# Output projection moved into the recurrence, two token norms merged into their neighbours by halves, in a convolution, recurrence, attention and experts kernel

## The chip, the cores and the metric

The kernel runs on one core of one Trainium2 chip. A core has five engines with a queue each: PE (matrix products into PSUM, 8 banks of 512 fp32 columns by 128 partitions), DVE (vector), ACT (scalar functions), POOL (general, slow), and SP, which issues the DMAs. They meet only through semaphores. The metric is the device time in microseconds of one execution; lower is better. Three runs of the kernel before gave 5703.51, 5706.22 and 5708.03, median 5706.22.

## What is computed

Four images (B = 4) of 128 channels by 64 x 64 positions (L = 4096 tokens, C = 128). Cut to what matters here:

```
order   = patches (4 x 4 pixels, 256 of them) sorted by a score from two convolutions
x1      = x in that order, plus a position table;  x1n = layernorm(x1)
xm, z   = x1n @ in_proj.T                  (256 channels each)
xc      = silu(causal conv over 4 tokens of xm)
h[t]    = exp(dt[t] A) * h[t-1] + dt[t] B[t] xc[t]      (256 x 16 states)
y[t]    = (sum over states h[t] C[t] + D xc[t]) * silu(z[t])
out_m   = y @ out_proj.T                   (128 channels), put back in the image's order
t1      = x + out_m                        (residual, tokens by channels)
q, k, v = layernorm(t1) @ W_qkv;  q and k normed over the tokens
t1      = t1 + softmax(10 q k.T) v @ W_out + b_out      (4 heads of 32)
out     = t1 + experts(layernorm(t1))      (8 experts, best 2 by router)
```

## The kernel before, in words

`program` runs `setup` once and then a loop over the four images. The body is a row of blocks: `score_and_sort`, `project`, `scan`, `unsort`, `qkv`, `attention` with `attention_out`, `ffn`. At a block's end `k.clear` is a barrier of all engines that also clears the semaphores, so nothing of one block overlaps the next. All data of an image lies in SBUF, in one arena of 44032 fp32 columns, at hand-written offsets; the order of work on each engine is written out by hand.

**`scan`** is the recurrence: 8 chunks (`NCH`) of 512 tokens (`CH`), 16 states each (steps s = 0 to 15), two halves of 128 channels. In a step PE spreads row B of the state over all partitions (L967, bf16, bank 0), may do some side work (`side`: parts of softplus for the next chunk, and `lend`, L922, which spreads B early for states 3, 6 and 10), spreads row C of two steps earlier (L919, bank 1), and adds the state of six steps earlier to y by identity matmuls (`total`, L913, banks 6 and 7; at its state 0 the D term comes first, L911). ACT writes exp(dt A) into banks 3 to 5 (L1004), saves the last column of a state (L1007), copies C (L990) and the lent rows (L996). DVE makes dt x B (`inject`, L1098), which reads bank 0, and runs the scan proper (L1122), two per step, one injection between them. POOL multiplies the states by C (L1067) in a ring of 8 buffers, and makes the injections of the three lent states (L1056). `finish` (L1104, DVE) multiplies y by silu(z), in place in `sz`, in step 4 of the following chunk, and after everything for the last one. Bank 2 (`X_BANK`) is shared by the side work. An fp32 matmul is two passes in the profile, one instruction each; a bf16 matmul and a transpose are one. All queues are in order.

**`unsort`**: SP loads the image anew (2 MB). PE projects y to 128 channels in 32 token tiles, two fp32 matmuls each, y being the stationary operand with a stride of 16 columns (L1171); ACT copies the eight banks to `om` (L1191). POOL puts the image into patch order (L1163). Then PE, for each of the eight groups of four tiles, applies the transposed permutation (two matmuls of 512 columns, L1179) and adds the image by four matmuls with the identity (L1183), which makes them tokens by channels; it waits for all of `om` first. DVE copies a group to `t1` (L1197) and takes the statistics of its four tiles (`tile_stats`, L1208).

**`qkv`** begins with `normalize`: DVE aggregates 32 tiles (L1225), adds eps (L1227), ACT takes the root (L1222), DVE the reciprocal (L1229) and then all 32 normalised tiles (L1232); PE transposes them (L1279), ACT copies the eight banks to `tnt` (L1315). When all are there PE starts on k and q (L1289), ACT keeping and squaring each (L1319, L1320).

**`attention_out`**: PE projects the output by channels (L1645), ACT adds the bias as it copies (L1657), PE transposes (L1650), DVE adds to `t1` (L1663) and takes the statistics (L1208). **`ffn`** begins with the same `normalize` and transposes (L1757), copies (L1811), then router (L1764, L1814, L1770), gates (L1838 to L1862, DVE) and experts (L1777, added by L1872).

## Time and profile before

| what | value |
|---|---|
| median of three runs | 5706.22 us |
| profiled execution: its time, its span | 5710.99 us, 5708.9 us |
| granted clock over the span | 0.943 |
| busy over the span: PE, DVE, ACT, POOL | 4840.9, 4925.1, 3936.4, 1610.3 us |
| first image: recurrence | 205 to 667 us |
| first image: unsorting, then norm up to the first key projection | 667 to 720, 720 to 733 us |
| first image: rest of `qkv`, attention | 733 to 784, 784 to 1321 us |
| first image: `attention_out`, `ffn` | 1321 to 1345, 1345 to 1440 us |

A line of the order of time gives start, duration, engine, line, operation, output<-input, count and, in brackets, how long the engine had been idle and who released it. A line of a stretch gives each engine's busy time and PEclk, the share of TensorE's full clock (2.4 GHz) that was granted. The images follow each other some 1430 us apart and look alike, so one of them is read.

### The profile page before, as it was taken

The numbers are of one execution on the slowest core, as the hardware profiler recorded it, in microseconds if no ns is written. First come the engines' busy times: TensorE is split into PE (matmuls) and PEld (weight loads), VectorE is DVE, ScalarE is ACT, GpSimd is POOL, SyncE is SP. The second block draws the span as 40 slices with busy tenths as digits, with TensorE's granted clock in tenths as the row PEclk, the third lists the DMA queues.
The fourth block names the chain that finished last, engine by engine and source line by source line (L and its number), as shares of the span: only waits on it lengthen the run. The fifth ranks groups of instructions, "written<-read, shape, count | busy, mean of one in ns | idle before, by whom it ended". The sixth has DMA issues, their size and how long they took to land. (4 is left out here: it accounts for less than half of the span.)

```text
span 5708.9 us, 100723 instructions
## 1 busy us (share of the span) xinstructions
PE 4840.9 (85%) x34256; PEld 2049.1 (36%) x34328; DVE 4925.1 (86%) x6398; ACT 3936.4 (69%) x5625; POOL 1610.3 (28%) x790
## 2 busy tenths in 40 slices
PE   5788879998788887999878887799986888879997
PEld 2333433333333343333433334333343333433334
DVE  6799679998789967999868996799986899679998
ACT  3777468993477837999347783789924777379992
POOL 1488500000048850000004884000000588400000
PEclk9899989999889998999988999899988899989998
DMA  1000020000000002000000000200000000020000
GB/s 40 0 1 0 15 64 9 9 5 23 23 0 1 0 15 64 9 9 5 23 23 0 1 0 15 64 9 9 5 23 23 1 1 0 15 64 9 9 5 15
DMA packets 41638, 87.27 MB, mean 15 GB/s; under 512 B 11672, under 2 KB 27872, under 8 KB 38112
## 3 DMA queue, kind: packets, MB, share of 16 engines
q1 hardware_dynamic: 41184, 81.11, 5.3%
q8 instruction: 298, 4.88, 0.4%
q14 instruction: 156, 1.28, 0.1%
HBM read 26.55 MB, written 8.39 MB: 6 GB/s over the span
## 5 line engine op out<-in xcount | busy, mean ns | idle before, releaser
L1483 ACT ACTIVATE arena<-ps 128x1024 f32<-128x1024 f32 x2048 | 1913.4, 1033 | 196.9 <-PE ps L1446 183.7
L1512 DVE TENSOR_TENSOR arena<-arena 128x1024 f32<-128x1024 f32 x1664 | 1901.5, 1216 | 35.0 <-ACT arena L1483 34.4
L1122 DVE TENSOR_TENSOR_SCAN arena<-ps,hlast,arena 128x512 f32<-128x512 f32 x1024 | 1251.3, 1265 | 26.5 <-ACT hlast L1007 12.1
L1067 POOL TENSOR_TENSOR arena<-arena 128x1024 f32<-128x1024 f32 x512 | 1200.7, 2355 | 241.0 <-ACT arena L990 173.0
L1446 PE MATMUL ps<-arena 128*32 128x512 f16 x16384 | 1097.4, 384 | 124.7 <-issue 46.7
L1429 PE MATMUL ps<-arena 128*32 128x512 f32 x8192 | 1071.3, 601 | 7.6 <-ACT arena L1483 3.9
L913 PE MATMUL ps<-arena,ident 128*128 128x512 f32 x2048 | 965.4, 595 | 1.1
L1004 ACT ACTIVATE ps<-arena,amat 128x512 f32<-128x512 f32 x1024 | 705.1, 689 | 372.2 <-DVE arena L1122 365.3
L1446 PEld LDWEIGHTS ps<-arena 128*32 128x32 f16 x16384 | 468.3, 98 | 982.1 <-issue 640.9
L1826 POOL MEMSET arena<- 128x1024 f32 x4 | 3.8, 952 | 2646.1 <-POOLq L101 2646.1
L1098 DVE TENSOR_TENSOR arena<-arena,ps 128x1024 f32<-128x1024 f32 x416 | 497.2, 1195 | 86.1 <-remote 62.6
L913 PEld LDWEIGHTS ps<-arena,ident 128*128 128x128 f32 x2048 | 392.3, 192 | 345.3 <-issue 316.6
L1429 PEld LDWEIGHTS ps<-arena 128*32 128x32 f32 x8192 | 212.4, 109 | 417.7 <-ACT arena L1483 237.3
L990 ACT ACTIVATE arena<-ps 128x512 f32<-128x512 f32 x512 | 297.0, 580 | 14.0 <-PE ps L919 11.9
L1872 DVE SCALAR_TENSOR_TENSOR arena<-ps,arena 128x128 f32<-128x128 f32 x1024 | 274.0, 342 | 1.6 <-PE ps L1777 0.2
L967 PE MATMUL ps<-arena,sel 128*128 128x512 bf16 x376 | 149.4, 397 | 147.9 <-DVE arena L1098 142.6
L1777 PE MATMUL ps<-expw,arena 128*128 128x512 f32 x512 | 250.9, 616 | 12.2 <-DVE arena L1841 8.3
L919 PE MATMUL ps<-arena,sel 128*128 128x512 bf16 x480 | 189.1, 394 | 83.0 <-ACT arena L990 79.0
L486 PE MATMUL ps<-arena 128*128 128x512 f32 x512 | 233.5, 617 | 18.3 <-DVE arena L346 18.3
L1056 POOL TENSOR_TENSOR arena<-arena 128x1024 f32<-128x1024 f32 x96 | 226.6, 2360 | 8.6 <-ACT arena L996 8.6
L602 PE MATMUL ps<-arena,ident 128*128 128x512 f32 x448 | 222.7, 610 | 0.4
L1416 PE MATMUL ps<-arena,ones 128*32 128x512 f32 x1536 | 203.6, 603 | 2.9 <-DVE arena L1512 1.7
(257 smaller groups left out, 4578.5 us busy)
## 6 DMA issues: line engine op xcount, KB each, us to landing
arena<-x SPq DMA_DIRECT2D x32, 512.0 KB, 5.2
arena<-arena SPq DMA_DIRECT2D x64, 256.0 KB, 6.0
arena<-arena SPq DMA_DIRECT2D x64, 224.0 KB, 5.8
arena<-arena SPq DMA_DIRECT2D x28, 512.0 KB, 3.5
arena<-pe SPq DMA_DIRECT2D x256, 32.0 KB, 1.8
out<-arena SPq DMA_DIRECT2D x8, 1024.0 KB, 3.9
expw<-L_ffn_expert_w SPq DMA_DIRECT2D x1, 512.0 KB
wqkv<-L_attn_W_qkv SPq DMA_DIRECT2D x1, 192.0 KB
```

Source lines behind the costliest of these rows:

```text
L913: last = pe.matmul(k.bank(Y_BANK + h), k.ident[:, :], halves(hb[s % RING])[:, h, :], start=False, stop=s == DS - 1)
L990: act.activation(cs[s % 4], k.bank(C_BANK), ACT.Copy).then_inc(cs_s, 1)
L1004: act.activation(da(s, h), halves(dt[q])[:, h, :], ACT.Exp, scale=k.amat[:, h, s:s + 1]).then_inc(da_s, 1)
L1067: pool.tensor_tensor(halves(hb[s % RING]), halves(hb[s % RING]), cs[s % 4].unsqueeze(1).broadcast_to([128, HD, CH]), ALU.mult).then_inc(hc ...
L1098: dve.tensor_tensor(halves(dbx[(q + owned(s)) % 2]), halves(u[q]), k.bank(B_BANK).unsqueeze(1).broadcast_to([128, HD, CH]), ALU.mult).then ...
L1122: dve.tensor_tensor_scan(halves(hb[s % RING])[:, h, :], da(s, h), halves(injected)[:, h, :], k.hlast[:, s, h, :], ALU.mult, ALU.add).then_ ...
L1429: last = pe.matmul(k.ps[32 * h:32 * h + 32, O * CH:(O + 1) * CH], v[:, j * 128 + 32 * h:j * 128 + 32 * h + 32], probs[(2 * j + h // 2) % 8 ...
L1446: last = pe.matmul(k.ps[32 * t:32 * t + 32, (2 * group[p] + e) * CH:(2 * group[p] + e + 1) * CH], ks[:, h, j * 128 + 32 * t:j * 128 + 32 * ...
L1483: act.activation(probs[p % 8], k.bank(2 * group[p], 2 * CH), ACT.Exp, scale=SCALE / SPLIT ** 2).then_inc(exp_s, 1)
L1512: dve.tensor_tensor(acc[p % 2], acc[p % 2], probs[p % 8], ALU.add).then_inc(acc_s, 1)
L1777: pe.matmul(k.bank(expert_bank(i, hb)), tnt[:, i * 128:(i + 1) * 128], k.expw[:, hb * HE:hb * HE + HE, :].rearrange("p e c -> p (e c)"), s ...
L1872: dve.scalar_tensor_tensor(tile, k.bank(expert_bank(i, hb), C, e * C), gate[:, i, hb * HE + e:hb * HE + e + 1], tile, ALU.mult, ALU.add).t ...
```

## The change

Three parts. First, `scan` projects each finished chunk to 128 channels itself: in step 12 of the next chunk, PE in bank 2, ACT back into `sz`; the last chunk after all sums. The lend of state 3 moves from step 13 to 14, ACT's copies of the lent states 3 and 6 to between the two exponentials of steps 14 and 15. Second, `unsort` only transposes the projected chunks (32 transposes with the strided columns as the stationary operand), and takes in the norm that `qkv` had. Groups go in the order 0, 4, 1, 5, 2, 6, 3, 7, so that each merge needs only two banks of `om`. The norm goes in two halves of 16 tiles; of each half DVE normalises the even tiles and ACT the odd ones (as x times scale plus shift). Third, `attention_out` is gone: `ffn` multiplies the attention's output, as the stationary operand, by `W_out` straight into tokens by channels, with the bias added by a bf16 matmul of ones (three bf16 pieces of the bias in rows 0, 32 and 64), and norms by halves in the same way.

```diff
 setup:
-    ... col("L1_attn_b_out", C_BO)
+    for q in range(3):
+        late.append((bias32[32 * q:32 * q + 1, :], w["L1_attn_b_out"].rearrange("(a c) -> a c", a=1)))
-            sp.wait_ge(zeroed, 6)
+            sp.wait_ge(zeroed, 9)
+            dve.memset(k.ones16[:, :], 1.0).then_inc(zeroed, 1)
+            step = Chain(dve, k.sem("v_chain"))
+            dve.wait_ge(loaded, total)
+            step(dve.tensor_copy(bias16[0], bias32))
+            step(dve.tensor_tensor(rest, bias32, bias16[0], ALU.subtract))
+            step(dve.tensor_copy(bias16[1], rest))
+            step(dve.tensor_tensor(bias16[2], rest, bias16[1], ALU.subtract))
+            for q in range(3):
+                step(dve.tensor_copy(k.outb[32 * q:32 * q + 1, :], bias16[q][32 * q:32 * q + 1, :]))
 scan, tensor:
+            def project_out(c):
+                pe.wait_ge(fin_s, c + 2)
+                for h in range(HD):
+                    last = pe.matmul(k.bank(X_BANK), k.outw[:, h, :], sz[:, h, cols_of(c)], start=h == 0, stop=h == HD - 1)
+                last.then_inc(out_mm, 1)
+                if s == 12 and not first(c):
+                    if more:
+                        pe.wait_ge(dt_s, c * HD + 2 * HD)
+                    else:
+                        pe.wait_ge(lent_s, lent(c, LATER) + 1)
+                    project_out(c - 1)
-                if s == 13:
-                    pe.wait_ge(dt_s, c * HD + 2 * HD)
+                if s == 14:
+                    if first(c):
+                        pe.wait_ge(dt_s, c * HD + 2 * HD)
+                    else:
+                        pe.wait_ge(out_s, c)
                     pe.wait_ge(pc_s, c + 2)
                     lend(c + 1, 1 - q, EARLY)
...
+            pe.wait_ge(out_s, NCH - 1)
+            project_out(NCH - 1)
 scan, scalar:
+            def keep_projected(c):
+                act.wait_ge(out_mm, c + 1)
+                act.activation(sz[:, 0, cols_of(c)], k.bank(X_BANK), ACT.Copy).then_inc(out_s, 1)
+                            if more and s == 14:
+                                copy_lent(c + 1, 1 - q, EARLY)
+                            if more and s == 15:
+                                copy_lent(c + 1, 1 - q, SOON)
+                    if s == 12 and not first(c):
+                        keep_projected(c - 1)
-                    if s == 13:
-                        copy_lent(c + 1, 1 - q, EARLY)
-                    if s == 15:
-                        copy_lent(c + 1, 1 - q, SOON)
+            keep_projected(NCH - 1)
 unsort:
+    order = [PS * t + o4 for o4 in range(PS) for t in range(TT)]
 tensor:
-            for i in range(NT):
-                ... two matmuls of y by outw
-            pe.wait_ge(o_ev, NT // 4)
+            for g in order:
+                for j in range(4):
+                    first = (g // PS) * 128 * OFF + 4 * (g % PS) + j
+                    last = pe.transpose(k.bank(g, 128, 128 * j), projected[:, first:first + 127 * OFF + 1:OFF], k.ident[:, :])
+                last.then_inc(turned, 1)
+            def merge(n):
+                ... as before, after pe.wait_ge(o_ev, TT * (o4 + 1)) and pe.wait_ge(xp_s, n + 1)
+            def turn(n):
+                pe.wait_ge(tn_s, 2 * (n + 1))
+                pe.wait_ge(act_s, 2 * (n + 1))
+                ... four transposes
+            for n in range(NG - 2):
+                merge(n)
+            for n in range(NG // 2):
+                turn(n)
+            for n in range(NG - 2, NG):
+                merge(n)
+            for n in range(NG // 2, NG):
+                turn(n)
 scalar (after the eight copies to om):
+            for a in range(2):
+                half = slice(a * HALF, (a + 1) * HALF)
+                act.wait_ge(var_s, a + 1)
+                act.activation(rs[:, half], rs[:, half], ACT.Sqrt).then_inc(std_s, 1)
+                act.wait_ge(sh_s, a + 1)
+                for n in range(a * HALF + 1, (a + 1) * HALF, 2):
+                    i = tile_of(n)
+                    act.activation(cols(tn, i), cols(t1, i), ACT.Identity, bias=shift[:, n:n + 1], scale=rs[:, n:n + 1]).then_inc(act_s, 1)
+                for n in range(a * NG // 2, (a + 1) * NG // 2):
+                    g = order[n]
+                    act.wait_ge(tr, n + 1)
+                    act.activation(tnt[:, g * CH:(g + 1) * CH], k.bank(g), ACT.Copy).then_inc(tr_ev, 1)
 vector (keep: copy and statistics of a group; variances: 16 aggregations and eps;
 normalise: reciprocal, shift, 8 tiles):
+            for n in range(4):
+                keep(n)
+            variances(0)
+            keep(4)
+            normalise(0)
+            for n in range(5, NG):
+                keep(n)
+            variances(1)
+            normalise(1)
 qkv: the norm, its 32 transposes and eight copies are gone
 attention_out: gone
 ffn, tensor:
+            for g in range(NG):
+                pe.matmul(k.bank(g).rearrange("p (i c) -> p i c", i=4), k.ones16[:, :], k.outb[:, :].unsqueeze(1).broadcast_to([128, 4, C]),
+                          start=True, stop=False)
+                for i in range(4):
+                    at = g * CH + 128 * i
+                    last = pe.matmul(k.bank(g, 128, 128 * i), ao[:, at:at + 128], k.wout[:, :], start=False, stop=i == 3)
+                last.then_inc(o_mm, 1)
+            for a in range(2):
+                ... four groups of four transposes, then the router of this half
 ffn, scalar: as in unsort, and each half's logits copied before the next half
 ffn, vector (residual: add to t1 and statistics of a group):
+            for g in range(4):
+                residual(g)
+            variances(0)
+            residual(4)
+            normalise(0)
+            for g in range(5, NG):
+                residual(g)
+            variances(1)
+            normalise(1)
```

## Rows read from the trace of the kernel before

**Rows 1.** Stretch of the recurrence: length, busy time of each engine, clock.
```profile
205.00:667.00 462.00, 379.37 (x926) 154.00 (x944) 430.19 (x368) 343.00 (x640) 385.81 (x176) 0.96 0.00 0
```

**Rows 2.** Order of time, end of the recurrence and unsorting.
```profile
665.22 1.23 DVE L1104 TENSOR_TENSOR arena<-ps,arena 128x1024 f32<-128x1024 f32 x1 [8.45 <-PE ps L913]
...
667.64 28.18 PE L1171 MATMUL ps<-outw,arena 128*128 128x128 f32 x128 [2.45 <-PEq L101]
...
676.13 8.51 POOL L1163 COPY arena<-arena 128x512 f32<-128x512 f32 x8 [15.54 <-DMA arena<-x]
...
696.50 1.98 PE L1179 MATMUL ps<-arena,permt 128*128 128x512 f32 x4 [0.69 <-ACT arena L1191]
...
698.32 1.05 PE L1183 MATMUL ps<-ident,arena 128*128 128x128 f32 x8
...
717.68 0.69 DVE L1197 COPY arena<-ps 128x512 f32<-128x512 f32 x1 [1.01 <-PE ps L1183]
718.41 0.87 DVE L1208 BATCH_NORM_STATS2 arena<-arena 128x6 f32<-128x128 f32 x4
```

**Rows 3.** Order of time, the norm ahead of the key projection.
```profile
720.49 2.22 DVE L1225 BATCH_NORM_AGGREGATE small<-arena 128x2 f32<-128x6 f32 x32 [1.21 <-PEq L101]
...
723.22 0.35 DVE L1229 RECIPROCAL small<-small 128x32 f32<-128x32 f32 x1 [0.29 <-ACT small L1222]
723.60 8.29 DVE L1232 TENSOR_SCALAR arena<-arena,small 128x128 f32<-128x128 f32 x32
...
732.31 0.60 ACT L1315 ACTIVATE arena<-ps 128x512 f32<-128x512 f32 x1 [0.43 <-PE ps L1279]
732.96 14.00 PE L1289 MATMUL ps<-arena,wqkv 128*128 128x512 f32 x32 [0.69 <-ACT arena L1315]
```

**Rows 4.** Order of time, from the attention's last division to the gates.
```profile
1320.73 0.69 DVE L1500 TENSOR_TENSOR arena<-arena 128x512 f32<-128x512 f32 x1
...
1322.87 8.81 PE L1645 MATMUL ps<-arena,wout 128*128 128x512 f32 x16 [5.60 <-PEq L101]
...
1332.15 0.69 DVE L1663 TENSOR_TENSOR arena<-arena,ps 128x512 f32<-128x512 f32 x1 [10.73 <-PE ps L1650]
...
1357.63 0.60 ACT L1811 ACTIVATE arena<-ps 128x512 f32<-128x512 f32 x1 [0.43 <-PE ps L1757]
...
1360.86 0.62 DVE L1838 COPY arena<-ps 128x128 f32<-128x128 f32 x2 [3.65 <-PE ps L1770]
```

**Rows 5.** Order of time in the recurrence, PE and DVE, around steps 9 to 13.
```profile
409.01 0.38 PE L967 MATMUL ps<-arena,sel 128*128 128x512 bf16 x1
...
409.44 1.88 PE L913 MATMUL ps<-arena,ident 128*128 128x512 f32 x4
411.15 1.88 PE L602 MATMUL ps<-arena,ident 128*128 128x512 f32 x4
...
418.67 0.38 PE L967 MATMUL ps<-arena,sel 128*128 128x512 bf16 x1
...
421.07 0.39 PE L967 MATMUL ps<-arena,sel 128*128 128x512 bf16 x1
...
423.30 1.19 DVE L1098 TENSOR_TENSOR arena<-arena,ps 128x1024 f32<-128x1024 f32 x1
...
602.33 3.27 PE L913 MATMUL ps<-arena,ident 128*128 128x512 f32 x4
```

**Rows 6.** Order of time, odd tiles normalised by ACT in the sorting block.
```profile
124.14 6.26 ACT L464 ACTIVATE arena<-arena 128x128 f32<-128x128 f32 x16 [2.90 <-DVE arena L402]
```

**Rows 7.** Stretches of the norm and of the attention's projection, columns as in rows 1.
```profile
724.00:726.00 2.00, 2.00 (x8) 1.45 (x8) 2.00 (x9) 0.60 (x1) 0.00 (x0) 0.50 0.00 0
730.00:732.50 2.50, 2.27 (x9) 1.14 (x9) 1.89 (x8) 1.38 (x3) 0.00 (x0) 1.00 0.00 0
1323.00:1325.00 2.00, 2.00 (x3) 0.96 (x4) 0.00 (x0) 0.05 (x1) 0.00 (x0) 0.50 0.03 8
```

**Rows 8.** Order of time in the setup, SP's queue: four row loads.
```profile
18.10 1.34 SPq L189 DMA_DIRECT2D expb<-L_ffn_expert_b  x4
```

More of the change, by code:

```diff
@@ L1175, in _ @@
-            pe.wait_ge(o_ev, NT // 4)
-            for g in range(NT // 4):
-                t, o4 = g // 4, g % 4
+            for g in order:
+                for j in range(4):
[4 more added lines that the diff above has]
+                g = order[n]
+                t, o4 = g // PS, g % PS
+                pe.wait_ge(o_ev, TT * (o4 + 1))
@@ L1185, in _ @@
                 last.then_inc(t_mm, 1)
+            def turn(n):
+                pe.wait_ge(tn_s, 2 * (n + 1))
+                pe.wait_ge(act_s, 2 * (n + 1))
+                for i in range(4 * order[n], 4 * order[n] + 4):
+                    last = pe.transpose(k.ps[:, i * 128:(i + 1) * 128], cols(tn, i), k.ident[:, :])
+                last.then_inc(tr, 1)
+            for n in range(NG - 2):
[4 more added lines that the diff above has]
+                merge(n)
@@ L1193, in _, with keep @@
         @block.vector
         def _(dve):
[L1195 to L1196 removed]
+            step = Chain(dve, k.sem("v_chain"))
+            def keep(n):
+                g = order[n]
+                dve.wait_ge(t_mm, n + 1)
                 dve.tensor_copy(t1[:, g * CH:(g + 1) * CH], k.bank(g)).then_inc(t_ev, 1)
[L1198 to L1208 removed]
@@ L1211, in normalize @@
[L1211 to L1233 removed]
+                dve.wait_ge(t_ev, n + 1)
@@ new lines, in keep, with variances @@
+                for m in range(4 * n, 4 * n + 4):
+                    dve.bn_stats(st[:, m, :], cols(t1, tile_of(m))).then_inc(st_s, 1)
+            def variances(a):
+                dve.wait_ge(st_s, (a + 1) * HALF)
+                for n in range(a * HALF, (a + 1) * HALF):
+                    dve.bn_aggr(mv[:, n, :], st[:, n, :]).then_inc(ag_s, 1)
+                dve.wait_ge(ag_s, (a + 1) * HALF)
+                half = slice(a * HALF, (a + 1) * HALF)
+                dve.tensor_scalar(rs[:, half], mv[:, half, 1], 1e-5, None, ALU.add).then_inc(var_s, 1)
@@ new lines, in normalise @@
+            def normalise(a):
+                half = slice(a * HALF, (a + 1) * HALF)
+                dve.wait_ge(std_s, a + 1)
+                step(dve.reciprocal(rs[:, half], rs[:, half]))
+                dve.scalar_tensor_tensor(shift[:, half], mv[:, half, 0], -1.0, rs[:, half], ALU.mult, ALU.mult).then_inc(sh_s, 1)
+                for n in range(a * HALF, (a + 1) * HALF, 2):
+                    i = tile_of(n)
+                    dve.tensor_scalar(cols(tn, i), cols(t1, i), mv[:, n, 0:1], rs[:, n:n + 1], ALU.subtract, ALU.mult).then_inc(tn_s, 1)
@@ L1276, in _ @@
         def _(pe):
-            for i in range(NT):
-                pe.wait_ge(tn_s, i + 1)
-                last = pe.transpose(k.ps[:, i * 128:(i + 1) * 128], tn[:, i * 128:(i + 1) * 128], k.ident[:, :])
-                if i % 4 == 3:
-                    last.then_inc(tr, 1)
             for m in (K_, Q_):
@@ L1713, in attention @@
     k.clear()
-    attention_out(k)
 def ffn(k, b):
@@ L1807, in _ @@
         def _(act):
-            normalize(k, None, act, TN_AT, T_AT, 1e-5)
-            for g in range(NG):
-                act.wait_ge(tr, g + 1)
-                act.activation(tnt[:, g * CH:(g + 1) * CH], k.bank(g), ACT.Copy).then_inc(tr_ev, 1)
             for a in range(2):
+                half = slice(a * HALF, (a + 1) * HALF)
+                act.wait_ge(var_s, a + 1)
+                act.activation(rs[:, half], rs[:, half], ACT.Sqrt).then_inc(std_s, 1)
+                act.wait_ge(sh_s, a + 1)
+                for i in range(a * HALF + 1, (a + 1) * HALF, 2):
+                    act.activation(tn[:, i * 128:(i + 1) * 128], t1[:, i * 128:(i + 1) * 128], ACT.Identity, bias=shift[:, i:i + 1],
+                                   scale=rs[:, i:i + 1]).then_inc(act_s, 1)
+                for g in range(4 * a, 4 * a + 4):
+                    act.wait_ge(tr, g + 1)
+                    act.activation(tnt[:, g * CH:(g + 1) * CH], k.bank(g), ACT.Copy).then_inc(tr_ev, 1)
                 act.wait_ge(k.sem("logits_t"), a + 1)
```

165 lines of the change are left out of this document (67 added, 98 removed).

## The prediction

> **What bounds the kernel now.** I read the busy time by stage first. In the recurrence DVE is busy 430 of 462 us, PE 379, POOL 386 [rows 1]: DVE sets the pace and PE has some 18% in hand. Then I read the order of time at the seams, where no engine is full and only the longest chain counts. From the recurrence's last gate (DVE, ends at 666.45) to the first key projection (732.96) 66.5 us pass, as four pieces in a row: a barrier of 1.2 us, 64 output projections on PE (28.2 us), eight merges (696.50 to 717.6) with the last statistics behind them (719.28) [rows 2], and after another barrier the norm: 2.4 us of aggregation and variance, the root, and 32 normalised tiles in 8.3 us with PE and ACT just behind [rows 3]. The second seam, from attention's last division (ends at 1321.42) to the gates' first copy (1360.86), takes 39.4 us: projection and transposes on PE, 12 us of residual and statistics on DVE (first at 1332.15), a barrier, the same norm, the router [rows 4]. Both seams come four times. The change touches these two and the recurrence.
>
> **Recurrence.** Added for each of 8 chunks: one two-step fp32 projection of 512 columns on PE and one copy on ACT. The ident sums beside it are two such matmuls and occupy PE 1.72 us between one bf16 spread and the next (1.88 with the drain); the copy is 0.60 [rows 5, 3]. For seven chunks it stands in step 12 ahead of the C spread and the sums. There the B spread of step 12 starts at 418.67, the next B spread at 421.07. Pushed back it starts at 418.67 + 0.21 + 1.72 + 0.21 + 1.72 = 422.5 and is readable 0.5 later at the most, 423.0. DVE takes it up at 423.30 [rows 5]. So DVE still covers it, with 0.25 us in hand; the step after has 0.9 us of slack on PE, and the lend that moves from step 13 to 14 gives 0.2 back. Cost taken: 0. If the cover is gone it is up to 1.72 us in each of 28 chunks, 48 us in all; below nothing I see no gain beyond 0.5 us a chunk from lent rows that ACT copies earlier, and DVE doesn't wait for those, so 0. ACT has idle time ahead of its exponentials, so the copies and the two moved ones cost nothing.
> The eighth projection has no cover: it waits for the last gate. 0.05 + 1.98 on PE + 0.6 on ACT = +2.7 us.
>
> **Unsorting and norm.** The block's PE work starts 2.7 us later, at 670.3. Gone are 128 passes at 0.22 us (28.2). In their place come 32 transposes that load the same strided columns, one load each: at 0.22 us 7.0 us, until 677.3. This price needs no better bound, since a wait comes after it: the image. POOL's first patch copy started 8.5 us after PE's first matmul and takes 1.06 [rows 2]; so the first patch is there at 670.3 + 9.55 = 679.9. That wait was hidden by the 28 us of projections and is now what is late: the first merge ends at 680.9. The next five at 2.61 each (20.9 us over eight): 694.0. DVE needs 1.6 per group (copy 0.69, statistics 0.87) and follows: four groups at 690.4, half the variances (16 of 32, 1.1 + 0.2 + gaps) at 691.8, the fifth group at 693.4, reciprocal and shift 0.6, 694.0. Then eight tiles on DVE (2.1) beside eight on ACT. ACT's tile is 0.39 us (16 in 6.26) against DVE's 0.26 [rows 3, 6], so the half takes 3.1: 697.2. PE turns the fourth group by 697.7 and only then does merges seven and eight, until 702.9; waiting here costs 3.7 us against merging straight on, as a price of the in-order queue. DVE ends the eighth group at 704.6, variances 706.0, root 706.3, shift 706.9, ACT's last tile 710.0, the four copies behind it on ACT (0.5 apart) 712.1, barrier 1.2: the key projection starts at 713.3 where it was 732.96. Gain 19.6.
> Bounds of this sum: nothing hidden better than here can save more than the wait for the image plus the 3.7 us in PE's queue; in the other direction a transposed group late by 1 us is late once, not eight times.
>
> **The clock at the key projection.** The clock stays at 2.4 GHz through merges seven and eight if transposes at this pace keep it there. In the norm of before PE had been idle since the last merge (717.6); the granted clock was 0.50 (1.2 GHz) while the first transposes ran, and by 730 to 732.5 it was 1.00, with nothing but transposes on PE [rows 7]. So transposes do raise it here. The Trainium skill, "TensorE: Matmul & The Clock Gate", Part 4: PE-mode transpose, says the opposite: that the full clock does not engage for transpose mode. By that rule the merges would begin at the low clock; what that gives is the third rival. But in the new order PE is idle from 702.9 to 707, turns 16 tiles, and is idle again until 713.3: the projections start at 1.2 GHz. A projection takes 1.7 us then against 0.86, ACT needs 1.06 for each, so the first two cost 0.8 and 0.7: -1.5. Bounds 0 to 3 us.
>
> **Second seam.** The block starts where the old one did, 1322.87. Per group PE issues a bf16 bias spread (0.21 at the full clock) and 8 passes of 128 columns (1.05) [rows 2, 5]; at the low clock that the first stretch has (0.50 in 1323 to 1325, rows 7), an estimate of twice that, 2.4. The first group is there at 1325.3, the second at 1327.3, and from then DVE is the bound at 1.5 per group (0.67 + 0.87): four groups 1331.9, variances 1333.4, fifth 1334.9, shift 1335.5, its tiles 1337.6, three groups 1342.1, variances 1343.6, root and shift 1344.5, ACT's tiles 1347.6, copies 1349.8. From the last such copy to the gates' first read it took 2.6 us; at the low clock, where PE now is after 6 us of little work, 3.1: 1352.9 against 1360.86. Gain 8.0. Bounds 7 (slow through the whole projection) to 10 (full clock throughout). What went is 8.8 us of PE, the copy by ACT, and a barrier of 2.2 us.
>
> **Setup, once.** One column load goes, three row loads come in SP's queue ahead of the image, at 0.34 us each [rows 8]: +0.7. The wait for nine zeroed tensors instead of six is met long before SP comes to it. DVE's seven small steps stand beside that image load.
>
> **Sum.** 19.6 - 1.5 + 8.0 = 26.1 a batch, 104 over four, less 0.7. The profiled execution took 5710.99 (span 5708.9); the median shown, 5706.22, is 4.8 lower. 5706 - 104 = 5602.
>
> **Rivals.** (A) PE is the bound in steps 10 to 14. For it: in these steps PE is nearly gapless and has 3.9 us of work for a step of 3.48; the margin is a quarter of a microsecond. Against it: the arithmetic above. DVE would lose 0.5 to 1.7 us in 28 chunks, 14 to 48 us: 5616 to 5650, 15%.
> (B) The slower side. The projection falls in stretches at the low clock: near 602 the same four passes took 3.27 us in place of 1.88 [rows 5]. Then the projection is 3.4, the sums 3.4, and B, C and POOL's ring of eight are late together in step after step. It decides from 104 / 28 = 3.7 us per chunk; a loss of 4.5 gives 5602 + 126 = 5728. Against it: a busier PE loses the full clock less, and this stretch is one at a chunk's seam. 3%.
> (C) Transposes don't hold the clock. Then the first and second merge, and the seventh and eighth, run 4 to 5 us at half speed and lose 2.3 each time: 4.6 a batch, 18: 5620. By the row above it is unlikely: 7%.
> (D) The change saves only the projection's time in part, since the image arrives later than before: DMA runs at the same rate, and nothing else uses it here; 2 us a batch, 5610, within my own range.
> Forecast 75%, A 15%, B 3%, C 7%.
>
> **Numbers.** 0.2% is 11 us, about what a measurement of this kernel can tell from no change. Forecast, C and half of A lie above 5580 and under 5635; the forecast's own range by the bounds (-3 to +2 us a batch at the seams, up to 0.3 us in 28 chunks) is 5588 to 5620. Low end 5582, high end 5635. Only B is slower; same would need A at its worst and C together with more, 1%.
>
> **What would show it.** In the profile after: PE's strided transposes some 7 us, then a POOL copy that PE waits for; ACT and DVE tiles side by side twice a block; no projection between scan and norm; the key projection 47 us after the last gate instead of 66.5; the gates 31.5 us after attention instead of 39.4; chunks of the recurrence as long as before. A chunk longer by over 0.5 us, with DVE's injection waiting for the B spread in step 13, means A. A first merge at a granted clock of 0.5 means C.

## The result, and the profile after

| | before | after |
|---|---|---|
| median of four runs | 5707.12 us | 5575.06 us |
| lowest and highest | 5703.51, 5710.72 us | 5571.39, 5584.34 us |
| profiled execution: its time, its span | 5710.99, 5708.9 us | 5571.39, 5569.7 us |
| granted clock over the span | 0.943 | 0.947 |

The ratio is 0.977 (95%: 0.9755 to 0.9784), a gain of 132 us. The forecast was 104 us (5602), with a low end of 5582. The direction and the mechanisms were forecast, the size was too small, and the time lies 7 us under the range. Between the two profiled executions the spans differ by 139.2 us, so that is the sum to be explained.

I cut both executions into the same nine pieces, by the start or end of fixed DVE instructions. The table gives the sum over four images, in us (the recurrence's first scan is the first scan instruction of DVE; the key maximum is the first reduction behind the key projection; "first sum copy" is DVE's first copy of an attention sum out of PSUM).

| piece | before | after | gain | forecast |
|---|---|---|---|---|
| setup | 39.3 | 39.8 | -0.5 | -0.7 |
| normalised image to first scan | 703.2 | 697.3 | 5.9 | 0 |
| first scan to last gate (recurrence) | 1808.2 | 1809.3 | -1.1 | 0 |
| last gate to first key maximum (first seam) | 277.5 | 204.8 | 72.7 | 72.4 |
| key maximum to first sum copy | 200.6 | 201.9 | -1.3 | 0 |
| first sum copy to last division (attention) | 2141.2 | 2117.2 | **24.0** | 0 |
| last division to gates' first copy (second seam) | 160.2 | 124.9 | 35.2 | 32 |
| gates to last expert | 314.8 | 311.2 | 3.6 | 0 |
| last expert to next image | 63.9 | 63.2 | 0.8 | 0 |

The three pieces that the change touches gave 106.8 us where 104.4 were forecast. The other 32 us came in pieces whose code is the same in both kernels. Both parts are read below.

**The first seam.** Order of time of the kernel after, first image (start, duration, engine, line, operation, tiles, count, and what ended the idle time before):

```profile
665.69 1.23 DVE L1147 TENSOR_TENSOR arena<-ps,arena 128x1024 f32<-128x1024 f32 x1 [10.12 <-PE ps L932]
667.07 1.96 PE L946 MATMUL ps<-arena,outw 128*128 128x512 f32 x4 [1.41 <-DVE arena L1147]
669.06 0.60 ACT L1030 ACTIVATE arena<-ps 128x512 f32<-128x512 f32 x1 [14.52 <-PE ps L946]
670.83 3.86 PE L1229 MATMUL ps<-ident,arena 128*128 128x128 f32 x32 [1.81 <-PEq L103]
...
680.46 1.98 PE L1241 MATMUL ps<-ident,arena 128*128 128x128 f32 x8 [4.05 <-POOL arena L1222]
...
682.23 2.77 PE L1237 MATMUL ps<-arena,permt 128*128 128x512 f32 x4
682.47 0.69 DVE L1285 COPY arena<-ps 128x512 f32<-128x512 f32 x1 [15.55 <-PE ps L1241]
...
702.66 0.69 DVE L1285 COPY arena<-ps 128x512 f32<-128x512 f32 x1 [3.09 <-PE ps L1241]
...
710.08 3.65 PE L1248 MATMUL ps<-ident,arena 128*128 128x128 f32 x16 [4.84 <-DVE arena L1305]
...
715.59 2.05 PE L1364 MATMUL ps<-arena,wqkv 128*128 128x512 f32 x2 [1.87 <-PEq L103]
```

The last gate ends at 666.92 and the key projection starts at 715.59: 48.7 us, against 66.5 in [rows 2, 3] and 46.9 forecast. Of the eighth projection (1.96) and its copy (0.60) nothing is hidden, as forecast. The 28.18 us of output projections are gone; 32 transposes stand there, in 3.86 us. Then PE waits 4.05 us for POOL's first patch, that is for the image. After this idle time the first merge's image part takes 1.98 us and the next spread 2.77, where the same shapes took 1.05 and 1.98 in [rows 2]. The stretches say why (length, then busy time of PE, PEld, DVE, ACT, POOL with counts, then the granted clock); the four lines are the transposes, the first merges of image 1, the same 3.8 us of image 3, and the start of the key projection in image 1:

```profile
670.80:674.60 3.80, 3.77 (x33) 3.80 (x34) 0.00 (x0) 3.05 (x7) 0.00 (x0) 1.00 0.65 193
...
680.12:683.92 3.80, 3.46 (x10) 2.44 (x11) 1.41 (x5) 0.00 (x0) 3.80 (x5) 0.56 0.02 4
...
3454.04:3457.84 3.80, 3.80 (x21) 2.83 (x22) 1.58 (x6) 0.00 (x0) 3.80 (x4) 1.00 0.02 4
...
715.60:719.00 3.40, 3.40 (x4) 1.47 (x5) 0.12 (x1) 1.17 (x3) 0.00 (x0) 0.50 0.02 5
```

In image 3 PE had waited 3.70 us for POOL's first patch and kept the full clock; the key projection starts 46.7 us after the gate, and at the full clock (5.82 us for its first thirteen passes). In the other three, after waits of 4.05, 3.82 and 4.16 us, the first merges are slow, the key projection starts after 48.7, 48.5 and 48.8 us, and at the low clock (3.75 for its first four passes). Up to the first key maximum it is 49.0 us in image 3 and 51.8 to 52.1 in the others.

**The recurrence.** Order of time, around step 12 of the same chunk as [rows 5]:

```profile
417.64 1.88 PE L946 MATMUL ps<-arena,outw 128*128 x4
...
419.36 0.38 PE L938 MATMUL ps<-arena,sel 128*128 128x512 bf16 x1
419.58 1.88 PE L932 MATMUL ps<-arena,ident 128*128 128x512 f32 x4
...
421.29 0.38 PE L1001 MATMUL ps<-arena,sel 128*128 128x512 bf16 x1
...
422.05 1.20 DVE L1141 TENSOR_TENSOR arena<-arena,ps 128x1024 f32<-128x1024 f32 x1
```

The projection, the C spread and the ident sums stand in a row, as forecast. The B spread starts at 421.29; with the 0.5 us until it can be read that is 421.8, and DVE takes it at 422.05 with no wait shown: the quarter of a microsecond that the forecast gave. Over the whole recurrence DVE is busy as long as in [rows 1], while PE has 6.3 us more, at a clock of 0.98 for 0.96:

```profile
205.00:667.00 462.00, 385.68 (x957) 159.23 (x973) 430.02 (x368) 345.43 (x647) 385.88 (x176) 0.98 0.00 0
```

**The second seam**, order of time, first image:

```profile
1299.83 0.69 DVE L1570 TENSOR_TENSOR arena<-arena 128x512 f32<-128x512 f32 x1
...
1302.37 1.91 PE L1803 MATMUL ps<-wout,arena 128*128 128x128 f32 x8
...
1304.32 0.69 DVE L1889 TENSOR_TENSOR arena<-arena,ps 128x512 f32<-128x512 f32 x1 [3.80 <-PE ps L1803]
...
1331.76 0.62 DVE L1927 COPY arena<-ps 128x128 f32<-128x128 f32 x2 [7.21 <-PE ps L1821]
```

From 1300.52 to 1331.76 it is 31.2 us; the forecast was 31.4, from 39.4 in [rows 4].

**The attention**, where the forecast had nothing. PE at its start, of the kernel before and of the kernel after; "issue" is time in which PE waited for nothing that the profile shows:

```profile
783.85 1.47 PE L1446 MATMUL ps<-arena 128*32 128x512 f16 x11 [16.30 <-issue]
789.44 5.49 PE L1446 MATMUL ps<-arena 128*32 128x512 f16 x53 [4.13 <-issue]
```

```profile
768.86 4.68 PE L1516 MATMUL ps<-arena 128*32 128x512 f16 x48 [16.39 <-issue]
```

Before, PE stops for 4.13 us after eleven matmuls of a stage whose code was not changed (3.00, 2.54 and 3.13 us in the other images). After, it runs through. The first of the eight chunks takes 73.8 to 75.1 us before, and 70.4 in all four images after. The third and the fifth chunk are also shorter, 67.3 and 67.2 us on average against 68.0 and 68.0; the rest are equal within 0.3.

### The profile page after: what moved, and what is told of

Read it like the earlier page. It is cut to its first block and busy times, and to the rows that moved or that the text cites. A ratio compares the mean times of both kernels' runs of the same rounds, so it can differ in the third digit from the quotient of the medians.

```text
span 5569.7 us, 100509 instructions
## 1 busy us (share of the span) xinstructions
PE 4759.2 (85%) x34096; PEld 1989.2 (36%) x34168; DVE 4895.4 (88%) x6312; ACT 3967.8 (71%) x5761; POOL 1610.1 (29%) x790
## 5 line engine op out<-in xcount | busy, mean ns | idle before, releaser
L1165 DVE TENSOR_TENSOR_SCAN arena<-ps,hlast,arena 128x512 f32<-128x512 f32 x1024 | 1253.8, 1271 | 26.0 <-ACT hlast L1047 11.6
L1141 DVE TENSOR_TENSOR arena<-arena,ps 128x1024 f32<-128x1024 f32 x416 | 499.6, 1201 | 75.2 <-remote 51.8
```

The costliest lines, as they stand in the source:

```text
L1141: dve.tensor_tensor(halves(dbx[(q + owned(s)) % 2]), halves(u[q]), k.bank(B_BANK).unsqueeze(1).broadcast_to([128, HD, CH]), ALU.mult).then ...
L1165: dve.tensor_tensor_scan(halves(hb[s % RING])[:, h, :], da(s, h), halves(injected)[:, h, :], k.hlast[:, s, h, :], ALU.mult, ALU.add).then_ ...
```

## Experiments

Single runs have a neighbour of the kernel before on the same chip; that one's time is given in brackets. Runs of before spread over 5703.5 to 5714.5, so I read the pieces inside the profiles, whose unchanged parts repeat within a few tenths, more than the totals.

### Is attention's gain the change's own?

The code of the attention is the same, but three things around it moved: the place of its instructions in each engine's stream, the addresses of the tensors in SBUF, and the time at which it starts.

**x1**: kernel before, 64 instructions that do nothing put into PE's stream, once, in the setup:

```diff
+        @block.tensor
+        def _(pe):
+            for _ in range(64):
+                pe.sem_inc(k.sem("pad"), 1)
```

> The kernel before, with 64 extra semaphore increments on PE in the setup, where PE has nothing to do; nothing else differs. Where the kernel after gained unforeseen is mostly attention: from its first sum copy to its last division 529.3 us an image instead of 535.3, and a stall of PE of 2.5 to 4.1 us (released by issue) just after the start is gone. Theory 1 (position of the instructions): attention's start falls elsewhere in PE's instruction stream; the stall of 3 to 4 us after the first few products goes or moves, attention comes to 530 to 532 us, in all four images alike, and the whole to 5685 to 5700. Theory 2 (SBUF addresses) and theory 3 (what the block before hands over: DMA and clock): attention stays at 534.3 to 536.7 with its stall, and the whole at 5704 to 5711.

5684.3 us (5707.3): 23 us are gained by 64 instructions that compute nothing. The attention takes 529.6, 529.6, 530.9 and 530.0 us, within a microsecond or so of the kernel after's (529.5, 528.9, 529.6, 529.2) and far from the kernel before's (535.4, 534.9, 536.7, 534.3): 21.2 us less in all, most of the 23. The gap in PE is gone:

```profile
784.74 4.62 PE L1451 MATMUL ps<-arena 128*32 128x512 f16 x48 [16.28 <-issue]
```

**x2**: kernel before with the SBUF tensors of the kernel after (two of them unused):

```diff
-        self.cols = sb("cols", [128, 64])
+        self.cols = sb("cols", [128, 32])
+        self.ones16 = sb("ones16", [128, 128], BF16)
+        self.outb = sb("outb", [128, C], BF16)
```

> The kernel before with the SBUF tensors of the kernel after (a smaller column table, two more bf16 tensors, not used), so that the arena lies at the other's address; no instruction differs. Theory 2 (addresses): attention falls from 535.3 to about 529.3 us an image, the whole to about 5685. Theories 1 and 3: attention 534.3 to 536.7, the whole 5704 to 5711.

5704.6 us (5707.3), attention 535.6, 534.6, 533.8, 533.3, and the gap is there (4.07 us in the first image). The addresses don't do it.

**x3**: kernel after, with 128 such instructions in PE's setup.

> The kernel after with 128 extra semaphore increments on PE in the setup. Theory 1 (position): the stalls of PE by issue inside attention move; attention changes by over 1 us an image against 529.3, up or down, most likely back up toward 533 with a stall soon after its start. Theories 2 and 3: attention stays at 528.9 to 529.6. The seams stay as they are by every theory (last gate to first maximum of the keys 49 to 52.1 us, last division to the gates 31.2).

5606.3 us (5707.3). The attention is back at 536.5, 535.1, 534.8, 536.8, and the gap with it:

```profile
770.80 1.46 PE L1521 MATMUL ps<-arena 128*32 128x512 f16 x10 [16.25 <-issue]
776.49 5.75 PE L1521 MATMUL ps<-arena 128*32 128x512 f16 x54 [4.23 <-issue]
```

The change, with its attention in a place as bad as that of before, is worth 101 us. The forecast was 104.

**x9**, **x10**, **x11**: kernel before with 64 increments in POOL's setup stream, and with 128 and 256 in PE's.

```diff
             step(pool.memset(k.cols[:, C_ONE:C_ONE + 1], 1.0))
+            for _ in range(64):
+                pool.sem_inc(k.sem("pad"), 1)
```

> The kernel before with the 64 extra increments on POOL instead of PE. If it is PE's own instruction stream that has to lie well, attention stays at 533 to 538 us an image with its stall by issue, the whole at 5700 to 5711. If any change of the program's layout does it, attention comes to 530 and the whole to 5684, as with the 64 on PE.

> The kernel before with 128 increments on PE. By the position theory the stall at attention's start stays away over a range of positions: with 64 it was gone; with 128 attention is 529 to 531 us again, the whole about 5685. Rival: 64 was a lucky draw, and any number gives a random value between 529 and 537.

> The kernel before with 256 increments on PE. The trace's DMA rows have instruction packets of 16384 bytes for the queue that serves PE; if an instruction takes 64 bytes these are 256 instructions, and attention's start lies at the same place of a packet as in the kernel before: the stall of 3 to 4 us just after the first products comes back, attention 533 to 537 us, the whole 5700 to 5715. Rival (what counts is only that something was put in): 529 to 531, 5685.

| kernel | time | attention, four images | PE's gap, first image |
|---|---|---|---|
| before | 5711.0 | 535.4, 534.9, 536.7, 534.3 | 4.13 |
| 64 on PE (x1) | 5684.3 | 529.6, 529.6, 530.9, 530.0 | none |
| 128 on PE (x10) | 5692.4 | 532.5, 529.6, 530.0, 531.5 | none |
| 256 on PE (x11) | 5711.7 | 533.7, 533.7, 536.0, 534.4 | 3.81 |
| 64 on POOL (x9) | 5710.5 | 534.6, 536.2, 532.6, 536.4 | 4.08 |

The neighbour of the last three took 5704.7. 256 instructions also lengthen the setup by 12.7 us, and x11 has two images in which another stage is 3.5 us shorter (it comes below), so its attention is read rather than its total. The attention of x10 lies a little above the 529 to 531 us expected in two images, without the gap. It is PE's stream and not POOL's, and a shift of 256 brings the bad place back, where 64 and 128 avoid it. The page of the kernel before has the queue that carries instructions:

```profile
q8 instruction: 298, 4.88, 0.4%
```

That is 4.88 MB in 298 packets, 16.4 kB each; x11, with 256 PE instructions more, has 299. So a stream comes in pieces of one size, and the experiments fit one in which 256 of PE's instructions are a piece. The times of the packets in the trace show what PE waits for. In every image of all 14 kernels, PE's first matmul of the attention's first chunk starts 1.5 to 1.8 us after a packet of this queue has landed, and a second one lands 2.3 to 4.2 us after that start. Seven kernels stop (before, x2, x3, x4, x5, x9 and x11, in all four images, 2.4 to 4.6 us), and each of these 28 stops ends 1.3 to 1.9 us after the second packet has landed. In the other seven it lands as late, and PE doesn't stop. Of the first image of before, from the stop at 785.32 to 789.44 (queue, then packets, MB and share of the 16 DMA engines; this q8 packet starts at 786.51 and has landed at 787.88):

```profile
q1 hardware_dynamic: 177, 0.85, 100.3%
q8 instruction: 1, 0.02, 2.1%
```

The attention's code stands behind a branch of PE's stream that jumps over the code of another variant. The hardware loop of the later chunks (`pe.Fori`) shows the same at its two jumps back: a stop by "issue" of 2.0 to 2.7 us at each, in every image of every kernel, 112 in all, each ending 1.6 to 1.9 us after a packet has landed. They are in both kernels and so don't tell them apart. So the gap is PE waiting for the next piece of its instructions behind a jump, and the place decides whether PE has enough instructions left to work through until it comes.

Whether the transfers that run at the same time make the piece late is open. Of the gap's own stretch the profile of before has (the last three numbers are clock, the DMA engines' busy share and GB/s):

```profile
784.00:792.00 8.00, 3.87 (x39) 1.17 (x32) 1.14 (x2) 2.53 (x3) 0.00 (x0) 0.50 1.03 210
```

The DMA engines are full. The second packet took 0.9 to 1.7 us (1.37 in this image); the 276 packets of this queue in before that had no transfer of q1 beside them took 0.99 at the median. That is some 0.4 us of a gap of 4.13. Whether the full engines also delay the packet's start isn't shown, and whether the gap goes when they are free wasn't tried.

### Which part of the change gave what?

**x4**: the third part alone on the kernel before: attention's projection by tokens in the block of the second norm, and that norm by halves.

```diff
-            for i in range(NT):
-                pe.wait_ge(tn_s, i + 1)
-                last = pe.transpose(k.ps[:, i * 128:(i + 1) * 128], tn[:, i * 128:(i + 1) * 128], k.ident[:, :])
...
+            for g in range(NG):
+                pe.matmul(k.bank(g).rearrange("p (i c) -> p i c", i=4), k.ones16[:, :], k.outb[:, :].unsqueeze(1).broadcast_to([128, 4, C]),
+                          start=True, stop=False)
...
-    attention_out(k)
```

> The kernel before with the third part of the change alone: attention's output projected straight into tokens and the second norm by halves; recurrence, unsorting and first norm as before. My sum: last division to the gates 31.2 us instead of 39.4 to 40.6, so 8 to 9 us an image; last gate to first maximum unchanged at 69 to 70. If the parts add, 35 us in all from this seam: 5672 plus what attention does. Theory 3 (hand-over from unsorting and norm): attention stays near 535, since its neighbour ahead is unchanged. Theory 1: attention may move to anything from 529 to 536, the PE stream ahead of it being what it was, it should stay near 535 too, unless the setup's few instructions matter.

5674.7 us (5707.3). The second seam takes 31.3, 31.1, 30.5 and 30.4 us, 9.2 less than before on average, and the first stays at 68.9. The experts behind it take 77.8 us once and 79.4 to 79.5 three times; with them the part is worth 8.9 us an image (118.7 to 109.9), with none of the rest of the change. The attention keeps its gap (2.4 to 4.2 us) and its length (534.4 to 538.1 us), as it should: in the stream of PE nothing ahead of it was changed.

**x5**: kernel after, but the output projection back in the unsorting block, with the recurrence as before; the norms by halves stay.

```diff
-                if s == 12 and not first(c):
...
-                    project_out(c - 1)
...
-                    last = pe.transpose(k.bank(g, 128, 128 * j), projected[:, first:first + 127 * OFF + 1:OFF], k.ident[:, :])
+                    for h in range(HD):
+                        last = pe.matmul(k.bank(g, 128, 128 * j), y[:, h, first:first + 127 * OFF + 1:OFF], k.outw[:, h, :],
+                                         start=h == 0, stop=h == HD - 1)
```

> The kernel after, but with the recurrence of before and the 64 strided projections in the unsorting block in place of the 32 transposes (the first part of the change undone, the halves kept). By the sum: the first group reaches DVE some 17 us later than in the kernel after (28.2 us of projections instead of a wait for the image), less 1 us because no merge runs at the low clock; last gate to first maximum 68 us, thus almost all of that seam's gain of 17 to 20 us an image is the projection's move, and the norm by halves gives only 1 to 2 us here. Rival: the halves give half of it, then the seam is 60. Whole 5638 to 5665, by where the longer PE stream puts attention's start.

5652.2 us (5707.4). From last gate to key maximum it takes 66.6 us in each image. Before it was 69.4 on average, after it is 51.2. So the halves alone give 2.8 us an image and the moved projection 15.4; the recurrence is 452.0 to 452.1 us without it, and 452.0 to 453.0 after. This kernel has a gap by issue of its own, of 4.60 us, after seven matmuls and so ahead of attention's first copy. Instructions were taken out of the stream again, and the place differs from both:

```profile
783.14 1.04 PE L1494 MATMUL ps<-arena 128*32 128x512 f16 x7 [16.30 <-issue]
788.78 4.22 PE L1494 MATMUL ps<-arena 128*32 128x512 f16 x41 [4.60 <-issue]
```

**x12**: kernel after, each output projection in the recurrence done twice (the second writes the same result).

```diff
-                for h in range(HD):
-                    last = pe.matmul(k.bank(X_BANK), k.outw[:, h, :], sz[:, h, cols_of(c)], start=h == 0, stop=h == HD - 1)
+                for _ in range(2):
+                    for h in range(HD):
+                        last = pe.matmul(k.bank(X_BANK), k.outw[:, h, :], sz[:, h, cols_of(c)], start=h == 0, stop=h == HD - 1)
```

> The kernel after with the projection in the recurrence done twice over (the second time over the first, same result). The forecast had the one projection covered with 0.25 us in hand at the B spread of step 13. Twice, this spread comes 1.72 us later, so DVE's injection is late by 1.72 - 0.25 = 1.5 us in each of seven chunks: 10 us an image, the recurrence from first scan to last gate 462.5 instead of 452.1, the whole 40 us longer plus 1.8 us an image at the uncovered eighth: 5620 to 5625. Rival: PE's slack of 12 us a chunk takes it up and the recurrence stays below 454: 5583.

5659.4 us (5704.7). The recurrence takes 463.6, 459.2, 463.6 and 459.2 us, 7.1 to 11.6 more than after. DVE, in the same place as above, now waits:

```profile
429.47 1.22 DVE L1142 TENSOR_TENSOR arena<-arena,ps 128x1024 f32<-128x1024 f32 x1 [1.38 <-PE ps L1002]
```

1.72 us more on PE cost 1.38 at DVE, so about 0.3 us was free; the forecast's margin was 0.25. Seven such chunks make 9.7 us; the recurrence grew by 9.1 on average. The total is 34 us higher than the upper end expected, for other reasons. One is 27.5 us more in the attention over four images, where the third and the fifth chunk take 70.1 to 70.8 us in place of 67.3. Its code wasn't touched either, only moved in PE's stream, and it has no gap at its start. The stage ahead of the first scan and the experts, untouched too, took 11.9 us more. The seam grew by 4.0 us an image, of which the second tail projection explains 1.7; the rest stays open.

### What is late in the first seam now?

**x6**: kernel after, all eight merges ahead of the first turning of tiles on PE:

```diff
-            for n in range(NG - 2):
+            for n in range(NG):
                 merge(n)
-            for n in range(NG // 2):
-                turn(n)
-            for n in range(NG - 2, NG):
-                merge(n)
-            for n in range(NG // 2, NG):
+            for n in range(NG):
                 turn(n)
```

> The kernel after with PE doing all eight merges before the first turn. If the order of PE's queue (merges seven and eight behind the first half's turns) costs what the forecast said, DVE's waits of 3.1 and 1.0 us for these merges go and the seam from last gate to first maximum falls by 3.5 to 4 us an image, to 48 on average: 5560. Rival: the first half's turns and copies then come late and are in front of ACT's second half: no gain. No PE instruction is added, so attention should stay at 529 to 530 us.

**x7**: kernel after, the image for the unsorting loaded in the recurrence's last chunk, when its place is free:

```diff
         def _(sp):
             steps.credit_first(sp)
+            sp.wait_ge(y_mm, (NCH - 1) * DS + 1)
+            for i in range(4):
+                sp.dma_start(k.at(i * 1024, 1024), k.ins["x"][b, :, i * 1024:(i + 1) * 1024]).then_inc(k.sem("x_in"), 16)
+            sp.wait_ge(k.sem("x_in"), 64)
...
-            pool.wait_ge(x_in, 64)
```

> The kernel after with the image loaded in the last chunk of the recurrence, once the D term has read the conv output that lies there. If the wait for the image is what starts the merges, 4.05 us of PE idle time and the low clock of the first merge (2.77 instead of 1.88, and the 1.98) go: seam 5 to 6 us shorter an image, 5552. Rival: the load disturbs the recurrence (its last chunk gets longer) or POOL's copies are the next wait, then under 2 us.

**x8**: both.

> Both of the two edits before. If they are independent waits on one chain they add up: seam 9 to 10 us an image shorter than in the kernel after, 5537, range 5530 to 5550. Rival: with the merges starting earlier DVE (1.6 us a group against PE's 2.6) hides one of the two, then 5552.

| kernel | time | last gate to key maximum, four images |
|---|---|---|
| after | 5575.1 | 52.0, 51.8, 49.0, 52.1 |
| merges first (x6) | 5563.0 | 48.0, 47.2, 48.8, 47.0 |
| image early (x7) | 5558.7 | 46.0, 46.0, 46.0, 46.0 |
| both (x8) | 5533.7 | 41.3, 42.1, 42.1, 42.1 |

The merges' place in PE's queue is worth 3.5 us an image (51.2 to 47.8), the image 5.2; both together 9.3. The totals of x6 and x7 fall by less, since pieces that weren't edited moved against them: against the profiled execution of after, the attention takes 3.9 and 5.9 us more and the experts 3.4 each. Order of time of x8, first image:

```profile
670.42 8.64 POOL L1220 COPY arena<-arena 128x512 f32<-128x512 f32 x8 [11.46 <-SPq L1216]
670.44 3.85 PE L1227 MATMUL ps<-ident,arena 128*128 128x128 f32 x32 [1.81 <-PEq L103]
...
674.13 1.88 PE L1235 MATMUL ps<-arena,permt 128*128 128x512 f32 x4
...
675.85 1.05 PE L1239 MATMUL ps<-ident,arena 128*128 128x128 f32 x8
676.74 1.88 PE L1235 MATMUL ps<-arena,permt 128*128 128x512 f32 x4
...
695.21 0.69 DVE L1279 COPY arena<-ps 128x512 f32<-128x512 f32 x1 [0.51 <-PE ps L1239]
```

POOL starts with PE's first transpose instead of 8.5 us after it, PE doesn't stop, and the merges behind the 32 transposes run at the full clock from the first on. The recurrence isn't longer (452.9, then 452.0), so the transfer under its last chunk costs nothing. Over four runs x8 takes 5529.6 to 5534.6 us, median 5533.74, a ratio of 0.9695 to the kernel before (0.9678 to 0.9711). It is the fastest version here; its interval doesn't meet that of the kernel after.

## Why the prediction was right and where it failed

**Recurrence: right.** Cost taken 0, measured 1.1 us over four images, of which 0.9 in the first alone. The margin of 0.25 us at the B spread of step 13 was a sum from rows, not a wait that they show; x12 measured it, at about 0.3. Rival A (15%) would have shown DVE waiting there, and did so only once PE's work was doubled. Rival B (3%) fell with it.

**First seam: right in sum, with one term far off that was hidden and one missing.** The transposes were priced at the strided load of the old projection, 0.22 us; they took 0.12 each, 3.86 us for 32. The forecast said that this price needs no better bound, since a wait for the image comes after, and so the 3.1 us went into that wait: 4.05 us, where the forecast's own times leave 0.7 (677.3 plus a spread of 1.9, until 679.9). What it missed is the clock behind the longer idle time: the key projection came 48.7, 48.5 and 48.8 us after the gate for 46.9, and 46.7 in image 3, the one that kept the full clock. That is about 2 us an image for three images. In the sum this is hidden, and that is luck. The key projection starts 18.4 us earlier on average (66.5 to 48.2) where 19.6 were forecast. Against that, the low clock there was to cost 1.5, counted against a kernel before at the full clock. Up to the first maximum it costs 0.2 on average (2.8 to 3.1), since two of the four images of before (2 and 3, granted clock 0.53; seam 69.8 and 69.9 us for the 68.9 of the image that was read) had it already. 18.4 - 0.2 is 18.2, and 19.6 - 1.5 is 18.1. The price of 3.7 us for the order on PE's queue was confirmed (3.5 by x6).

**Clock at the key projection: right in kind, in three images of four.** 1.5 us was taken; the projections start at a granted clock of 0.50 in three images of four, and by the pieces that costs 0.9 us up to the first maximum (in the first image 3.29 us, against 2.37 before and 2.34 in image 3) and 0.3 an image in the next piece.

**Rival C: its loss occurred, its mechanism didn't.** The first merge was to run at the low clock because transposes don't hold it. It did, in three images, but the granted clock during the transposes is 1.00, it was 1.00 too behind a wait of 3.70 us in image 3, and in x7 and x8, with no wait between the transposes and the merges, no merge is slow (granted clock 1.00 over all merges of all four images). So it is the idle time. The Trainium skill's statement ("TensorE: Matmul & The Clock Gate", Part 4: PE-mode transpose) that the full clock does not engage for transpose mode doesn't hold for these runs.

**Rival D: right in kind.** It put 2 us an image on the later load; x7 gains 5.2 when the load is early, the clock's part included.

**Second seam: right**, 8.8 us an image for 8.0 (31.2 for 31.4 in the first image; before had 40.0 on average, not the 39.4 of the first image that was read). 2.4 of the 3.2 us beyond the forecast thus come from reading one image for four.

**The step that failed is the last line of the sum**, "5706 - 104": it takes every piece that isn't touched as unchanged. No term and no rival stood for them, and the range was built from the bounds of the touched pieces alone. The others gave 32.4 us together: besides the three below, +0.8 between the images, -1.3 behind the key maximum and -0.5 in the setup.

- The attention, 24.0 us. x1 gets 21.2 of it from the kernel before with 64 empty instructions, x3 loses it again from the kernel after with 128. It isn't an effect of what the change computes, only of how many PE instructions stand ahead. The first chunk is 15.3 us of it over four images; its gaps, in which PE waits for instructions, add up to 12.8. Another 6.0 us are the third and fifth chunks; why they take 0.75 us less each isn't known.
- The piece ahead of the first scan, 5.9 us. At its end stand the projections of the last three chunks on PE. The first of the three takes 3.78 us in every image, and the two behind it run at either clock with the same work. Order of time of the two kernels in their second image:

```profile
1620.55 3.78 PE L711 MATMUL ps<-arena,xpw 128*128 128x512 f32 x4 [1.90 <-ACT arena L742]
1626.24 3.78 PE L711 MATMUL ps<-arena,xpw 128*128 128x512 f32 x4 [1.90 <-ACT arena L742]
```

```profile
1593.22 1.98 PE L729 MATMUL ps<-arena,xpw 128*128 128x512 f32 x4 [1.90 <-ACT arena L760]
1597.10 1.98 PE L729 MATMUL ps<-arena,xpw 128*128 128x512 f32 x4 [1.90 <-ACT arena L760]
```

  The idle time ahead of each is the same 1.90 us. From the first convolution tap to the first scan it takes 61.7 us at the low clock and 58.3 at the full one. It was short in no image of before, in three of after, in one of x1 and x7, in two of x8, in none of x3, x4 and x12. The 3.4 us are not all gained. In those three images of after, the first twelve passes of the same stage take 7.08 us at a granted clock of 0.76, where before they take 5.39 at 1.00, and the taps start 1.6 us later. So the piece is shorter by 1.0, 1.9 and 1.5 us in these three images, not by 3.4. In image 3, where neither level differs, it is shorter by 1.5 us too, 1.4 of it ahead of the first projection. Over all 56 images of the 14 kernels the two go together: the 12 with the slow start all have the short end, of the other 44 only four. It shifts with no edit to it. What picks the level isn't settled.
- The experts, 3.6 us: 77.8 or 79.6 us an image, two long ones before and none after, but two in x7 and three in x12. This is the clock too. Stretches of the kernel before, in image 1 (77.8 us) and in image 3 (79.6 us): each time from the gates' first copy to DVE's first addition of an expert, then the 9.1 us behind.

```profile
1360.86:1370.68 9.82, 7.11 (x12) 2.79 (x12) 8.62 (x22) 0.97 (x2) 0.00 (x0) 0.83 0.00 0
1370.68:1379.79 9.11, 7.61 (x27) 3.80 (x28) 8.99 (x34) 1.02 (x1) 0.00 (x0) 1.00 0.01 2
4203.07:4212.89 9.82, 5.42 (x12) 2.20 (x12) 8.62 (x22) 0.97 (x2) 0.00 (x0) 1.00 0.00 0
4212.89:4222.00 9.11, 8.63 (x21) 4.03 (x22) 9.00 (x34) 1.02 (x1) 0.00 (x0) 0.63 0.01 2
```

  A low clock in the first of the two stretches costs nothing, the first addition comes 9.82 us behind the copy either way; in the second it costs 1.6 to 1.9 us. In 32 of the 56 images the granted clock over those 9.82 us was under 0.9, and all 32 took 77.8 us. The other 24 took 79.4 to 79.7, but for three at 78.0. When the clock falls isn't settled here either.

With the attention in its bad place and the stage of the last projections at its long value in all images, x3 stands at 5606, four microseconds from the forecast. The forecast of the change's own work was right, and the range left out what a change does by its length.

## What to carry to other kernels

Compare the pieces that a change doesn't touch as well as those it does: in a kernel of long streams with jumps, 64 empty instructions in one engine's stream moved the total by 23 us, so a padded version of the kernel before is the control that a gain of that size needs. In a forecast, give such a kernel's range a term for it, when the profile shows gaps by "issue" at the start of a loop. Where work is removed that hid a load, look at once for the earliest time at which that load may start: here it was worth more (5.2 us an image, with the clock that the idle time cost) than the shorter norm of the same block (2.8).

## What of the hardware was not expected

- PE's instruction stream has good and bad places. The first chunk of a stage behind a jump stalled for 2.4 to 4.6 us a few matmuls behind its start in seven kernels (before, x2, x3, x4, x5, x9, x11). The profile names no semaphore for it ("issue"), but each stall ends 1.3 to 1.9 us after an instruction packet of 16.4 kB has landed. In the kernel before, padding by 64 or 128 removes it, by 256 brings it back.
- Each jump back of PE's loop in the attention cost a stop of 2.0 to 2.7 us, in every kernel.
- 32 transposes of fp32 tiles that load a strided stationary operand took 0.12 us each (3.86 us), where a projection pass over the same columns took 0.22 (28.18 us for 128).
- After idle times of 3.7 to 4.2 us PE came back at either clock: full after 3.70, low after 4.05, mixed after 3.82 and 4.16 (granted 0.69 over the next 3.8 us).
